# One core, adaptive attention and GRU: an opening shared out over four engines, key transfers ahead of V's, four buffers for V's rows

## The reference, cut to what matters

```python
scale, shift = split(cond @ W_emb + b_emb)
xn  = rms_norm(x, g_norm) * (1 + scale) + shift
q, k, v = split(xn @ W_qkv)                    # 16 heads of 16
q, k = rms_norm(q, g_q), rms_norm(k, g_k)
o = softmax(q k^T / 4) v
x = x + o + o @ W_out
# GRU over the 32 steps, initial state cond, input x, W_ih, W_hh, biases
x = x + GRU(cond, x)
```

## Time and profile before

| what | us |
|---|---|
| median of 3 runs | 360.34 (359.83 to 360.48) |
| the profiled execution | 359.24 |
| its span, first to last instruction | 357.4 |
| PE busy in the span | 336.6 (94%) |
| DVE, ACT, POOL busy | 251.8, 228.5, 204.8 |
| mean granted clock of PE | 0.989 |

### The profile page before, as it was taken

The page is one execution under the profiler, slowest core; times in us unless marked ns, Lnnn a source line. Parts: engine busy times, 40 slices in busy tenths (PEclk is TensorE's granted clock), DMA queues, the critical chain, the costliest instruction groups (busy, mean ns, idle before and its releaser), DMA issues.

```text
span 357.4 us, 12902 instructions
## 1 busy us (share of the span) xinstructions
PE 336.6 (94%) x4314; PEld 306.2 (86%) x4314; DVE 251.8 (70%) x637; ACT 228.5 (64%) x668; POOL 204.8 (57%) x381
## 2 busy tenths in 40 slices
PE   7788799999999999999789999999999999999990
PEld 6567688888888888888578999999999999999990
DVE  3668699999999999999875555555655555655554
ACT  4677578888888888876545565555555555565441
POOL 5587577877778777877522445444345444445330
PEclk9999899999999999999999999999999999999997
DMA  6962554322222223222310011111111111111122
GB/s 198 329 198 76 148 153 131 86 71 83 82 83 69 80 83 85 79 74 81 84 33 2 9 29 27 29 29 26 26 27 26 28 28 27 26 26 27 29 31 30
DMA packets 54800, 24.91 MB, mean 70 GB/s; under 512 B 40802, under 2 KB 49652, under 8 KB 54772
## 3 DMA queue, kind: packets, MB, share of 16 engines
q1 hardware_dynamic: 53492, 22.16, 25.3%
q10 hardware_dynamic: 1280, 2.39, 2.1%
HBM read 7.48 MB, written 4.19 MB: 33 GB/s over the span
## 4 chain that ended last, share of the span: by engine, by line
PE 81%; SPq 7%; DMA 3%; DVE 2%; POOL 2%; issue 2%; ACT 1%; POOLq 0%
PE bank L1048 38%; PE bank L1100 24%; PE bank L1207 4%; PE bank L1188 4%; PE bank L1176 4%; SPq L388 3%; SPq L380 3%; DMA operands<-operands 2%; PE bank L1159 2%; PE bank L1168 2%; DMA vec_rows<-in_L_cond_g_k_dram 1%; PE bank L1113 1%; PE bank L1054 1%; POOL operands L447 1%; POOL xn L458 0%
## 5 line engine op out<-in xcount | busy, mean ns | idle before, releaser
L1100 PE MATMUL bank<-h,w_hh_sb 128*128 128x128 f32 x768 | 95.0, 278 | 0.2
L1100 PEld LDWEIGHTS bank<-h,w_hh_sb 128*128 128x128 f32 x768 | 90.8, 191 | 1.9 <-issue 0.5
L1020 DVE SCALAR_TENSOR_TENSOR operands<-bank,vec_cols,operands 128x128 f32<-128x128 f32 x64 | 22.2, 347 | 47.1 <-ACT operands L767 47.1
L1048 PE MATMUL bank<-pair_hi,wih_hi 128*128 128x256 f32 x180 | 52.8, 293 | 0.0
L767 ACT ACTIVATE operands<-bank,bsum 128x128 f32<-128x128 f32 x64 | 22.9, 358 | 46.4 <-PE bank L1100 45.2
L544 POOL TENSOR_TENSOR operands<-operands,h 128x128 f32<-128x128 f32 x64 | 29.5, 462 | 38.5 <-ACT operands L768 38.5
L1048 PE MATMUL bank<-pair_lo,wih_hi 128*128 128x256 f32 x180 | 50.4, 280 | 0.0
L1048 PE MATMUL bank<-pair_hi,wih_lo 128*128 128x256 f32 x180 | 50.3, 280 | 0.0
L553 POOL TENSOR_TENSOR operands<-h,x2T 128x256 f32<-128x256 f32 x31 | 22.5, 725 | 46.8 <-issue 34.2
L1048 PE MATMUL bank<-wqkv_hi,xn_hi 128*128 128x256 f32 (+1 forms) x126 | 47.9, 380 | 0.4 <-POOL xn_lo L476 0.3
L1048 PE MATMUL bank<-wqkv_lo,xn_hi 128*128 128x256 f32 (+1 forms) x126 | 42.8, 340 | 0.0
(11 more groups left out here) (125 smaller groups left out, 849.7 us busy)
## 6 DMA issues: line engine op xcount, KB each, us to landing
v_diag<-v_rows SPq DMA_DIRECT2D x128, 34.0 KB
operands<-operands SPq DMA_DIRECT2D x64, 64.0 KB, 2.0
operands<-operands SPq DMA_DIRECT2D x32, 128.0 KB, 2.1
out_dram<-operands SPq DMA_DIRECT2D x254, 16.0 KB, 1.4
x_in<-in_x_dram SPq DMA_DIRECT2D x7, 512.0 KB, 8.3
stage_w<-in_L_cond_W_ih_dram ACTq DMA_DIRECT2D x2, 384.0 KB, 3.7
w_hh_sb<-in_L_cond_W_hh_dram ACTq DMA_DIRECT2D x2, 384.0 KB, 3.6
w_emb_sb<-in_L_cond_W_emb_dram ACTq DMA_DIRECT2D x1, 512.0 KB, 4.5
```

The costliest lines, as they stand in the source:

```text
L1020: dve.scalar_tensor_tensor(out=rh[:, c, :], in0=xnh[:, HN_COL:HN_COL + B], scalar=bhh[:, 2 * KC + c:2 * KC + c + 1], in1=r_g[:, c, :], op0 ...
L1048: last = pe.matmul(dst, a, w, start=start and i == 0, stop=i == len(terms) - 1, skip_group_check=True)
L1100: last = pe.matmul(dst, gate(w_hh_sb, name, c)[k], moving, start=k == 0 and (name == "n" or opens and name == "z"), stop=k == KC - 1, skip ...
```

## The change

SP places keys before V in each turn. `v_rows` has four slots, each with its own semaphore, and ACT's copy of V no longer waits for a V transfer. The shifts go from DVE to ACT, between the xhats of groups 0 and 1, and read a bank of their own; the conditioning products signal scales and shifts apart. Weight chunk 1 is rounded and subtracted on POOL ahead of its pipeline, chunk 0's rounding on ACT moves ahead of the copy of the vectors. The second pair's four norm instructions go from POOL (turn 3) to DVE (turn 2), its squares stay in ACT's turn 1 and its logarithm and exponential go to turn 2. Group 0's V products take high by high and low by high first and wait for the weights' low part only at the third term. The unread transposes go from 11, 3 and 8 to 14, 5 and 12.

```diff
-        v_rows = sb("v_rows", [P, 2, HEADS, VW])
+        v_rows = sb("v_rows", [P, 4, HEADS, VW])
...
-        v_diag_ready = [sem("v_diag_ready0"), sem("v_diag_ready1")]
+        v_diag_ready = [sem(f"v_diag_ready{i}") for i in range(4)]
...
@@ sync: body
+                g = group(base, u, SP_KEYS)
+                if g is not None:
+                    place_keys(g, (u - SP_KEYS) % 2)
                 v = group(base, u, SP_V)
                 if v is not None:
-                    place_values(v, (u - SP_V) % 2, (u - SP_V) % 4)
-                g = group(base, u, SP_KEYS)
-                if g is not None:
-                    place_keys(g, (u - SP_KEYS) % 2)
+                    place_values(v, (u - SP_V) % 4)
...
@@ gpsimd: body
-                if turn_is(base, u, POOL_XLO):
-                    second_norms()
...
@@ gpsimd: ahead of the pipeline (second_norms' four instructions leave)
+            pool.wait_ge(qk_loaded[1], 16)
+            pool.tensor_copy(wqkv_hi[:, 1, 0:2 * D], stage_w[:, 1, 0:2 * D]).then_inc(wqk_hi_ready[1], 1)
+            pool.wait_ge(wqk_hi_ready[1], 1)
+            pool.wait_ge(first_norm, 6)
+            pool.tensor_tensor(wqkv_lo[:, 1, 0:2 * D], stage_w[:, 1, 0:2 * D], wqkv_hi[:, 1, 0:2 * D].bitcast(F32),
+                               ALU.subtract).then_inc(wqk_ready, 1)
...
@@ scalar: ahead of the pipeline
+            act.wait_ge(qk_loaded[0], 16)
+            act.copy(wqkv_hi[:, 0, 0:2 * D], stage_w[:, 0, 0:2 * D]).then_inc(wqk_hi_ready[0], 1)
             act.wait_ge(vec_ps, 1)
             act.copy(vec_cols[:, :], p_o[:, 0:20]).then_inc(vec_cols_ready, 1)
...
+            def shifts():
+                act.wait_ge(vec_cols_ready, 1)
+                act.wait_ge(emb_ps, 2)
+                for c in range(KC):
+                    last = act.activation(mod_shift[:, c, :, :].rearrange("p g b -> p (g b)"),
+                                          p_s[:, BANK + c * B:BANK + c * B + B], ACT.Identity,
+                                          bias=bemb[:, KC + c:KC + c + 1])
+                last.then_inc(mod_ready, 1)
...
@@ scalar: values
-                if later(v, 2):
-                    act.wait_ge(v_diag_ready[slot], spread(v - 2, slot, GB))
...
@@ scalar: body
                 if turn_is(base, u, ACT_XHAT):
+                    shifts()
                     scaled_input(1, 1)
-                    projection_weights(1)
-                    second_norms()
+                    second_squares()
...
                 if turn_is(base, u, ACT_XN):
+                    second_norms()
                     value_weights()
...
@@ vector
-            def shifts_and_gains():
...
-                for c in range(KC):
-                    projection_weights(c)
+            def weights_and_gains():
+                projection_weights()
...
+            def second_norms():
+                second = [norm_first[:, i, FIRST_PAIR:FIRST_NORMED] for i in range(7)]
+                dve.wait_ge(rs0_ready, LAG_QK)
+                dve.tensor_tensor(second[4], second[3], second[3], ALU.mult).then_inc(second_norm, 1)
...
...
@@ tensor
-            keep_busy(p_qk[1], 11)
+            keep_busy(p_qk[1], 14)
...
-            keep_busy(p_qk[1], 3)
+            keep_busy(p_qk[1], 5)
...
-            keep_busy(p_qk[1], 8)
+            keep_busy(p_qk[1], 12)
...
+            def first_value_projection():
+                pe.wait_ge(wv_hi_ready, 1)
+                terms = [(xn_hi, wqkv_hi), (xn_lo, wqkv_hi), (xn_hi, wqkv_lo)]
+                for i, (x_part, w_part) in enumerate(terms):
+                    if i == 2:
+                        pe.wait_ge(wv_ready, 1)
...
@@ tensor: attention_products
-                pe.wait_ge(v_diag_ready[slot], spread(g, slot, GB))
+                pe.wait_ge(v_diag_ready[place], spread_by_four(g, place, GB))
```

More of the change, by code:

```diff
@@ L188, in adaptive_attention_gru @@
         eps_ready = sem("eps_ready")
-        wqk_hi_ready = sem("wqk_hi_ready")
+        wqk_hi_ready = [sem(f"wqk_hi_ready{c}") for c in range(KC)]
         wqk_ready = sem("wqk_ready")
@@ L374, in _, with place_values @@
             sp.wait_ge(ones_ready, 2)
-            def place_values(v, slot, place):
+            def place_values(v, slot):
                 sp.wait_ge(v_ready, v + 1)
@@ L379, in place_values @@
                     rows = slice(T * b, T * b + T)
-                    sp.dma_start(v_diag[rows, place, b, :, :].rearrange("p h f -> p (h f)"),
+                    sp.dma_start(v_diag[rows, slot, b, :, :].rearrange("p h f -> p (h f)"),
                                  v_rows[rows, slot, :, :].rearrange("p h f -> p (h f)"))\
@@ L398, in body @@
                     place_keys(g, (u - SP_KEYS) % 2)
+                v = group(base, u, SP_V)
+                if v is not None:
+                    place_values(v, (u - SP_V) % 4)
                 if turn_is(base, u, SP_V):
@@ L664, in input_squares @@
                 act.wait_ge(ssx_ready, n)
-                act.wait_ge(rs_ready, n - 1)
+                if later(n, LAG_QK + 2):
+                    act.wait_ge(rs_ready, n - LAG_QK - 1)
                 act.sem_inc(square_x_free, 1)
@@ L693, in scaled_input @@
                     act.wait_ge(first_norm, 6)
+                elif first:
+                    act.wait_ge(second_norm, 4)
                 else:
-                    act.wait_ge(rs_ready, LAG_QK if first else n + 1)
+                    act.wait_ge(rs_ready, n - LAG_QK + 1)
                 if later(n, 2):
@@ L1061, in _ @@
             last.then_inc(condT_ps, 1)
-            keep_busy(p_qk[1], 3)
+            keep_busy(p_qk[1], 5)
             pe.wait_ge(condT_ready, 1)
             pe.wait_ge(emb_loaded, 16)
-            for m in range(2 * KC):
-                for c in range(KC):
-                    last = pe.matmul(p_s[:, m * B:m * B + B], w_emb_sb[:, c, m * P:m * P + P], h[:, 1, c, :],
-                                     start=c == 0, stop=c == KC - 1)
-            last.then_inc(emb_ps, 1)
+            for part in range(2):
+                for m in range(KC):
+                    for c in range(KC):
+                        last = pe.matmul(p_s[:, part * BANK + m * B:part * BANK + m * B + B],
+                                         w_emb_sb[:, c, (part * KC + m) * P:(part * KC + m) * P + P], h[:, 1, c, :],
+                                         start=c == 0, stop=c == KC - 1)
+                last.then_inc(emb_ps, 1)
             pe.wait_ge(vec_loaded, 16 * 6)
             pe.transpose(p_o[:, 0:20], vec_rows[:, :], ident[0:20, 0:20]).then_inc(vec_ps, 1)
-            keep_busy(p_qk[1], 8)
+            keep_busy(p_qk[1], 12)
             def projection_input(slot):
@@ L1143, in query_key_products @@
                          [wqkv_lo[:, c, 0:2 * D] for c in range(KC)]).then_inc(qk_ps, 1)
+            def first_value_projection():
[4 more added lines that the diff above has]
+                        pe.wait_ge(wv_ready, 1)
+                    for c in range(KC):
+                        last = pe.matmul(p_v, x_part[:, 0, c * P:c * P + P], w_part[:, c, 2 * D:3 * D],
+                                         start=i + c == 0, stop=i + c == len(terms), skip_group_check=True)
+                last.then_inc(v_ps, 1)
             def value_projection(g, slot):
                 if isinstance(g, int) and g == 0:
-                    pe.wait_ge(wv_ready, 1)
+                    first_value_projection()
+                    return
                 if later(g, 1):
```

56 lines of the change are left out of this document (23 added, 33 removed).

## The result

The changed kernel took 358.21 us in the median of four runs (357.58 to 358.76), the kernel before 360.18 (359.83 to 360.48): a ratio of 0.9945, 95% interval 0.9925 to 0.9965. In a later set with more runs of each it was 358.64 against 359.60, a ratio of 0.9972 (0.9945 to 0.9999). By these two pairs of medians the change brings 1.0 to 2.0 us; 2.35 were forecast.

What follows compares the result with a forecast made beforehand. It took TensorE working without a break (81% of the chain) as the bound, with gains only in its waits in opening and drain; -3.25 + 0.9 = -2.35 from a median of 360.34 gave 358.0 us, range 355.5 to 360.2.

Steps and rivals of the forecast that it cites:

- The opening's hand-over, -1.38: Opening: moving shifts to ACT and norms to DVE was to start products 1 at 15.50 us, 1.38 earlier.
- Rival 3: Opening shortens less: POOL's weights or the norms hold it, products 1 only 0.5 us earlier, 358.8 us; chance 0.12.
- POOL's weights: Opening: weight chunk 1's copy from 7.5 us and subtraction done by 9.95, hidden until xmod(0) at 10.67; cost nothing.
- S(0) at 25.55: Opening: TensorE's scores of group 0 were to start at 25.55 us instead of 27.27, after keys 0 at 22.05.
- Stalls on SP: SP's long DMA issues follow PE code packets; first hidden, second adds 1.08 us to K(2), third 0.7 to V(4).
- Rival 1: No SP stall counts: opening 4.45 us earlier, drain costs 0, total 355.9 us; chance 0.17.
- S(4) 3.25 earlier: Attention loop: scores of group 4 start at 45.15 us instead of 48.41, and that lead stays.
- The half clock near 40 gone: TensorE's 3.2 us at half clock disappear, worth 1.6 us, if 1.3 us of idle time don't lower it.
- Rival 2: Half clock stays after a 1.3 us idle time before scores 2: 359.6 us; chance 0.17.
- V's buffers, 0: Four buffers remove ACT's wait for V transfers: gain 0, but they let V go behind K without stopping ACT.
- The drain, +0.9 of at most 1.4: Attention's end: V issues queued between K(28) and K(31) on SP delay K(31), costing 0.9 us, bounds 0 to 1.4.
- Rival 4: Slower through SP's queue: stalls hit opening key issues, clock drops, drain costs 1.4 us; 361.4 us; chance 0.10.

Runs made afterwards that it cites:

- a0: The changed kernel again, unedited, as reference for later runs: 358.64 us against 359.60 for the kernel before, ratio 0.9972.
- e1: Changed kernel with V ahead of the keys on SP again, opening and four buffers kept: measured as good as the whole change or better, no figure given.
- e2: Kernel before with keys ahead of V and four V buffers, without the new opening: ratio 1.0008 to the kernel before.
- e11: Changed kernel with only the new opening kept, V first and two V buffers: median 357.34 us, ratio 0.9938 to the kernel before.
- e4: Changed kernel with SP's load of the last four groups of x moved from turn 5 to 8: time no better, no figure given.
- e5: Changed kernel with 64 semaphore increments on PE ahead of its first unread transpose: 367.18 us against 358.93, ratio 1.0210.
- e8: Changed kernel with V(30)'s four transfers issued by ScalarE at the end of turn 36 instead of SP: 356.41 us against 358.56, ratio 0.9937.
- e10: Changed kernel with V's rows back in two buffers and ScalarE's copy waiting for V transfers again; new opening and order kept: ratio 1.0010.
- e6: Changed kernel with V first from turn 32 on and the last load of x in turn 8: ratio 1.0031.
- e7: Changed kernel with the unread transposes back at 11, 3 and 8: ratio 0.9955.
- e9: Changed kernel with V(30)'s transfers on ScalarE and unread transposes at 11, 3 and 8: 355.67 us, ratio 0.9922 to the kernel before.

## Why the prediction was right, and which terms were not

The time lay 0.2 us from the forecast, the difference of the medians (-1.97) 0.4 from the sum (-2.35). The direction and the opening's mechanism were right; that the number was hit so closely was luck. In the pair of traces both large terms were too friendly, by 0.9 and 1.0 us, the later set of runs (a0) has a difference of 0.96, and by e1, e2 and e11 the keys-first order, which the forecast priced as part of the gain, brings nothing that a time shows. Two things that the forecast did not know made the first pair of medians come out near it: the two executions traced lay 0.94 under and 0.55 over the medians of their runs, and the drain costs less in the other traces.

- **The opening's hand-over, -1.38: right.** From the first xhat to products 1 it was 16.88 - 9.04 = 7.84 us, now 6.47: -1.37, in the changed kernel and within 0.03 of it in eight of the ten other traces used here that have the new opening (e4: 6.61; e5, which holds PE up at its start: 7.51). Of this, 0.52 were earned up to products 0 (from 3.54 behind the first xhat to 3.02), where the shifts had been the last input, and 0.85 between products 0 and 1, where the norm instructions had stood. Products 1 came at 15.79 and not 15.50 because x came in 0.28 later. Rival 3 falls. No run takes the opening's moves apart, so what each is worth alone is read from these traces, not tested.
- **POOL's weights: mis-sized, and still hidden.** The copy began at 7.89, when the chunk landed, and not at 7.5. The subtraction took 1.28, outside my bounds of 0.61 and 1.04, and ended at 10.63, not 9.95; the cover until xmod's end was used up to 0.15 us. DVE's first two norm steps took 0.40 and 0.54 beside POOL's two-input work, the last two 0.16 each, and all four still ended before DVE's next demand. The Trainium skill, page "GPSIMD Engine Reference", section "Specifications", has GpSimd's SBUF interfaces shared with VectorE; the trace agrees, by those 0.40 and 0.54 against 0.16.
- **S(0) at 25.55: failed in this trace.** It came at 27.73. V(0) took 3.21, its first issue 1.31 of that with no packet near it; then the packet in the stretch of 19 us met the last input load (1.48), and K(0), issued as forecast within 0.3 us (22.29), landed behind that load. In e8 and e10, where the load was done before the packet came, scores 0 were at 25.24. I had placed the first packet in SP's idle time.
- **Stalls on SP: right in kind.** K(2) took 0.63 over 1.86, against 1.08 forecast, and 0.55 to 1.04 in a0, e4, e6, e8 and e10; the third hit K(4) (+1.01), not V(4). Rival 1, where no stall counts, falls. The Trainium skill, page "Runtime: NRT & Kernel Launch", section "Instruction fetch mechanics", calls the cost of crossing a 16 KiB boundary of code "mostly hidden"; for SP's queue the trace disagrees, by these numbers.
- **S(4) 3.25 earlier: mis-sized.** 2.38 here and 2.52 to 3.22 in the other traces with the same opening, order and unread counts. That the lead then stays was right here (2.22 at scores 28); a0 and e8 lost 0.9 and 0.8 of theirs on that way, and why is open.
- **The half clock near 40 gone: right**, in every trace used here that has the new opening (the drops in the table lie elsewhere); with the old opening (e2) it stayed, after a wait of 1.91. Rival 2 falls. But my reason, that a shorter wait keeps the clock up, is not borne out: e1 and e8 waited 1.78 and 1.93 ahead of scores 2 and had no drop there.
- **V's buffers, 0: right as a condition.** I gave them no gain of their own but made them what lets V go behind the keys; e10's time and its copies' waits agree with that, though its trace doesn't show the way from the waits to the time.
- **The drain, +0.9 of at most 1.4: the failed step.** It gave back 1.9, and 1.4 to 1.7 in a0, e4, e7 and e10. I counted 13.3 us from K(28) to K(31) plus the two stalls seen before, 1.5 together, and let half of the first fall into SP's wait. It was 177.81 - 162.28 = 15.53: two stalls, 1.18 and 1.03 over 1.86, both fell on keys, K(28) and K(29), with no wait left to hide in. And a third that I had not counted, 0.50, fell on K(31) itself, for which scores 31 wait; in a0, e4, e7 and e10 it was 0.66 to 1.24. In the kernel before, no issue of K(31) was long.

Rival 4, slower through SP's queue, named the right place and too high a price: e2, the order without the opening, loses 1.25 us in the drain and by its time is neither slower nor faster (0.9980 to 1.0036).

## What to carry to other kernels

When a queue's order is changed, price it at both ends of the loop: a queue with 0.6 us to spare per turn in the loop has none in the drain, where each group's issues stand in a row. Ask first whether another engine's queue is idle there: four issues moved to ScalarE kept 2.3 us of lead where 0.3 had been left. And compare traces by the lead at fixed points, with the median of the runs beside it; one trace against one trace would here have shown a gain of 0.4 us.

## What the runs showed of the hardware that I had not expected

A semaphore increment alone took 0.14 to 0.17 us of TensorE's time (e5). And the half clock doesn't follow the length of a wait: the drop near 40 came after waits of 1.82 (before) and 1.91 (e2) ahead of scores 2, yet e8 waited 1.93 there without one; behind scores 31 it came after 1.22 (e9), 1.97 (e4) and 2.36 (e10), and not after 1.22 (e8), 1.81 (changed kernel) and 2.16 (a0). Where it came there, scores 31 to the first GRU product took 11.8 to 12.2 us in place of 10.9 to 11.3.
